# A convolution and attention hybrid on one core: the spectral mixer's lag blocks, regrouped by half of the tokens

## The reference, cut to what matters

```python
# phi: (tokens, 16 filters), causal convolution of u with each filter k
U_plus  = causal_conv(phi[:, k], u)                 # (b, t, k, d)
U_minus = sgn * causal_conv(phi[:, k], u * sgn)     # sgn = +1, -1, +1, ...
out  = einsum('btkd,k,kde->bte', U_plus,  sigma**0.25, M_phi_plus)
out += einsum('btkd,k,kde->bte', U_minus, sigma**0.25, M_phi_minus)
out += sum(shift(u, i) @ M_u[i] for i in range(3))
```

## Time and profile before

| | us |
|---|---|
| median of 3 runs | 216.42 (215.61 to 217.93) |
| profiled execution, device time | 216.58 |
| its span (first to last instruction) | 214.8 |
| PE / DVE / ACT / POOL busy | 186.6 / 154.1 / 97.3 / 39.2 |
| mean granted clock of TensorE over the span | 0.96 of full speed |

### The profile page before, as it was taken

One profiled execution on the slowest core, in us unless ns is written; L12 is line 12 of the kernel. 1 busy time (PEld: TensorE's weight loads), 2 busy tenths in 40 slices (PEclk: granted clock), 3 DMA queues, 4 the chain that ended last, 5 costly groups with the idle time before them and its releaser, 6 DMA issues.

```text
span 214.8 us, 6817 instructions
## 1 busy us (share of the span) xinstructions
PE 186.6 (87%) x2969; PEld 136.4 (64%) x2969; DVE 154.1 (72%) x347; ACT 97.3 (45%) x239; POOL 39.2 (18%) x57
## 2 busy tenths in 40 slices
PE   7999989899997989974898798598499969979994
PEld 2677668899997889721344684244147737735993
DVE  2789997958999999869777166595768749646101
ACT  3734997478888778511003350200868510035100
POOL 4970000012421440540100301133000000110000
PEclk9999999999999999999699999969955999999999
DMA  6830426345455510000143140001200190000000
GB/s 180 285 117 5 154 95 201 107 133 197 150 158 166 180 49 3 4 0 5 22 159 99 27 110 0 0 5 32 67 25 3 25 366 22 0 0 0 3 0 24
DMA packets 9042, 17.07 MB, mean 79 GB/s; under 512 B 2504, under 2 KB 3752, under 8 KB 8884
## 3 DMA queue, kind: packets, MB, share of 16 engines
q1 hardware_dynamic: 8868, 16.34, 24.1%
q10 hardware_dynamic: 144, 0.30, 0.4%
HBM read 16.20 MB, written 0.42 MB: 77 GB/s over the span
## 4 chain that ended last, share of the span: by engine, by line
PE 57%; DVE 26%; issue 6%; ACT 5%; POOL 2%; DMA 2%; POOLq 1%; DVEq 0%
PE ps L1540 55%; DVE onehot L1068 5%; POOL rstd L578 2%; DVE dots L1094 2%; DMA cst<-in_cst 2%; DVE arena L453 2%; DVE att L1118 1%; ACT arena L641 1%; DVE stu_fq L1443 1%; ACT onehot L837 1%; ACT table L641 1%; ACT arena L858 1%; DVE dots L1100 1%; DVE arena L1524 1%; DVE arena L1048 1%
## 5 line engine op out<-in xcount | busy, mean ns | idle before, releaser
L1540 PE MATMUL ps<-table,onehot 128*128 128x64 bf16 x1728 | 52.9, 194 | 5.0 <-issue 2.8
L1540 PEld LDWEIGHTS ps<-table,onehot 128*128 128x128 bf16 x1728 | 51.5, 98 | 6.5 <-issue 4.8
L1540 PE MATMUL ps<-spare 128*128 128x512 bf16 (+1 forms) x128 | 36.6, 419 | 8.1 <-DVE rexp L1359 2.3
L725 ACT ACTIVATE arena<-ps 128x512 f32<-128x512 f32 (+1 forms) x40 | 21.5, 553 | 14.2 <-PE ps L1540 13.9
L1540 PEld LDWEIGHTS ps<-spare 128*128 128x128 bf16 x128 | 12.4, 109 | 24.4 <-issue 6.8
L453 POOL TENSOR_TENSOR arena<-arena,w4p 128x288 f32<-128x288 f32 x21 | 16.2, 803 | 57.9 <-DVE arena L453 57.8
L1540 PE MATMUL ps<-arena 128*32 128x66 f32 (+4 forms) x388 | 25.2, 281 | 0.2 <-DVE arena L1320 0.2
L1540 PEld LDWEIGHTS ps<-arena 128*32 128x32 f32 (+2 forms) x388 | 22.2, 156 | 4.1 <-issue 1.4
L578 POOL TENSOR_TENSOR rstd<-var_eps,cst 128x4 f32<-128x4 f32 (+2 forms) x9 | 8.8, 982 | 82.7 <-DVE var_eps L937 56.1
L641 ACT ACTIVATE arena<-ps 128x512 f32<-128x512 f32 (+3 forms) x16 | 7.0, 469 | 26.1 <-PE ps L1540 20.3
L1068 DVE TENSOR_SCALAR onehot<-indexb,cst 128x2304 bf16<-128x2304 bf16 (+1 forms) x24 | 17.7, 771 | 0.0
(11 more groups left out here) (280 smaller groups left out, 305.0 us busy)
## 6 DMA issues: line engine op xcount, KB each, us to landing
indexb<-index_rows SPq DMA_DIRECT2D x20, 288.0 KB, 3.3
stu_fq<-index_rows SPq DMA_DIRECT2D x8, 288.0 KB, 3.4
arena<-in_toep SPq DMA_DIRECT2D x1, 2120.5 KB, 9.6
l<-in_l SPq DMA_DIRECT2D x1, 646.5 KB
stu_fq<-in_stu SPq DMA_DIRECT2D x1, 560.0 KB, 3.8
onehot<-in_l3w SPq DMA_DIRECT2D x1, 512.0 KB
table<-stu_mixed SPq DMA_DIRECT2D x4, 128.0 KB, 2.2
l<-in_l SPq DMA_DIRECT2D x1, 384.0 KB, 7.3
```

The lines of the kernel that those rows point to most:

```text
L725: nc.scalar.activation(gv[:, b % 2, :, at:at + count, :], ps[:, SB[n % len(SB)], 0:count * SLOT].rearrange("p (s a d) -> p a s d", s=count ...
L1540: return nc.tensor.matmul(out_ap, lhsT, rhs, start=start, stop=stop)
```

## The change

- **Values.** `projected` writes them in another arrangement: the partitions hold two groups of 8 filters (s = 0, 1) by 64 tokens, the columns the early and the late half of the tokens by 8 filters. Instead of 4 products (32 rows x 128 columns of weights, 512 moving columns) there are 16 (32 rows x 64 columns of weights, 256 moving columns): two halves by two groups by four images. The same values reach the same banks, and the copies keep their shapes.
- **Early tokens.** One 128x128 block now holds two filters' 64 early rows, so ODD, EVEN and BOTH each take 8 products where they took 16.
- **Late tokens.** They reach late results only, through a 64-column slice of the block (the lags of late to late are those of early to early). `add_late` issues two products of 128 rows x 64 columns: pair j to the partitions 64 to 127 of bank 4, pair j+1 to the partitions 0 to 63 of bank 1 (`LATE_BANK`). 4 such pairs each for ODD, EVEN and BOTH.
- **Joining.** ScalarE copies bank 1 (64 x 256) to SBUF (`late_rows`, a new last step of `a6`), and a product with a 64x64 identity adds it to the upper partitions of bank 4, between BOTH and the taps.
- **`toep`** is half as large and comes by three DMAs instead of one.

```diff
--- before.py
+++ after.py
@@ -210,9 +210,11 @@
         taps_v = arena[:, 2048:2048 + K2 * P]
         taps_q, taps_k = (arena[:, 2048 + at * P:2048 + (at + K2 - TAPS) * P] for at in (K2, 2 * K2 - TAPS))
         warm = sb("warm", [P, 1])
+        PAIRS, EARLY = NF // 2, P // 2
         fk, vcs = arena[:, 0:4096], arena[:, 4096:4096 + T * HG * 4 * HCOLS]
         v_sum, v_diff = arena[:, 0:NF * N], arena[:, NF * N:2 * NF * N]
-        ar_v, toep = arena[:, 8192:8192 + KU * N], arena[:, 8960:8960 + NF * LAGS + XT]
+        ar_v, toep = arena[:, 8192:8192 + KU * N], arena[:, 8960:8960 + PAIRS * LAGS + P]
+        late_rows = arena[0:EARLY, 11264:11264 + N]
         att_ch, y1, x2, ctx_n, qc, kc, vt, ln_ch, x4d, x5p = (
             arena[:, 12416 + i * N:12416 + (i + 1) * N] for i in range(10))
         vt1 = arena[:, 14976:14976 + T * (C + 1)].rearrange("p (n c) -> p n c", c=C + 1)
@@ -343,8 +345,8 @@
         PROJECTED = ("diff_even", "sum_even", "sum_odd", "diff_odd")
         v6 = Steps(sem("vector_stu"), "sum0 cen0 sq0 var0 eps0 sum1 cen1 ln0 sq1 var1 eps1 ln1 rows1 taps2 taps3 "
                    + " ".join(f"{n}{b}" for n in PROJECTED for b in (2, 3)) + " x6a x6")
-        a6 = Steps(sem("scalar_stu"), "x5p0 x5p1 rows0 taps0 taps1 " + " ".join(f"{n}{b}" for n in PROJECTED for b in (0, 1)))
-        t6 = Steps(sem("tensor_stu"), "parity0 parity1 turn0 turn1 taps " + " ".join(PROJECTED) + " out")
+        a6 = Steps(sem("scalar_stu"), "x5p0 x5p1 rows0 taps0 taps1 " + " ".join(f"{n}{b}" for n in PROJECTED for b in (0, 1)) + " late")
+        t6 = Steps(sem("tensor_stu"), "parity0 parity1 turn0 turn1 taps " + " ".join(PROJECTED) + " late out")
 
         block = ctx.enter_context(nc.Block())
 
@@ -559,7 +561,10 @@
                 sp.dma_start(heads_of[1][second, :], turn_d[0:NHEAD, N:N + DH]).then_inc(d_den, 16)
 
             sp.wait_ge(t5.sem, t5["kv3"])
-            sp.dma_start(toep, toep_d).then_inc(d_toep, 16)
+            for s in range(2):
+                sp.dma_start(toep[s * EARLY:(s + 1) * EARLY, 0:PAIRS * LAGS],
+                             toep_d[0:EARLY, s * PAIRS * LAGS:(s + 1) * PAIRS * LAGS]).then_inc(d_toep, 16)
+            sp.dma_start(toep[:, PAIRS * LAGS:], toep_d[:, NF * LAGS:NF * LAGS + P]).then_inc(d_toep, 16)
 
             sp.wait_ge(v6.sem, v6["x6"])
             sp.dma_start(out, x6t).then_inc(d_out, 16)
@@ -890,6 +895,8 @@
                 act.wait_ge(t6.sem, t6[name])
                 for b in (0, 1):
                     copy(by_parity_and_image(values)[:, r, b], ps[:, banks[b], :].rearrange("p (k e) -> p k e", k=NF), a6, f"{name}{b}")
+            act.wait_ge(t6.sem, t6["late"])
+            copy(late_rows, ps[0:EARLY, 1, 0:N], a6, "late")
 
 
         @block.vector
@@ -2030,8 +2037,13 @@
             def projected(name):
 
                 _, r, at, banks = PLACES[name]
-                for b, rows in IMAGES:
-                    ins = mm(ps[:, banks[b], :], tokens[rows, r, :], stu_w[rows, at:at + NF * D])
+                filters = PAIRS * D
+                for half in range(2):
+                    for s in range(2):
+                        for b, rows in IMAGES:
+                            ins = mm(ps[s * EARLY:(s + 1) * EARLY, banks[b], half * filters:(half + 1) * filters],
+                                     tokens[rows, r, half * EARLY:(half + 1) * EARLY],
+                                     stu_w[rows, at + s * filters:at + (s + 1) * filters])
                 ins.then_inc(t6.sem, t6.step(name))
 
             def taken(name):
@@ -2052,22 +2064,42 @@
                 return mm(ps[:, 4, to], lags, values, **{"start": False, "stop": False, **kw})
 
 
-            pe.wait_ge(d_toep, 16)
-            for k in range(NF):
-                at = k * LAGS
-                if k == NF // 2:
+            def add_late(pair, to, lag, values, at, **kw):
+
+                for j, rows, bank in ((pair, slice(EARLY, P), 4), (pair + 1, slice(0, EARLY), LATE_BANK)):
+                    first = j * LAGS + lag
+                    value = values[:, (PAIRS + j) * N + at.start:(PAIRS + j) * N + at.stop]
+                    ins = mm(ps[rows, bank, to], toep[:, first:first + EARLY], value,
+                             **({"start": False, "stop": False, **kw} if bank == LATE_BANK else {"start": False, "stop": False}))
+                return ins
+
+            LATE_BANK = 1
+            pe.wait_ge(d_toep, 48)
+            for j in range(PAIRS):
+                at = j * LAGS
+                if j == PAIRS // 2:
                     taken("sum_even")
                     pe.wait_ge(a6.sem, a6["sum_odd0"])
                     projected("diff_odd")
-                add(ODD, toep[:, at + P + 1:at + LAGS], v_diff[:, k * N:k * N + P], start=k == 0)
+                add(ODD, toep[:, at + P + 1:at + LAGS], v_diff[:, j * N:j * N + P], start=j == 0)
             taken("sum_odd")
+            for pair in range(0, PAIRS, 2):
+                add_late(pair, ODD, P + 1, v_diff, EVEN, start=pair == 0)
             taken("diff_odd")
-            for k in range(NF):
-                at = k * LAGS
-                add(EVEN, toep[:, at + P:at + LAGS - 1], v_diff[:, k * N + P:(k + 1) * N])
-                add(BOTH, toep[:, at:at + P], v_sum[:, k * N:(k + 1) * N])
-
-            at, taps = NF * LAGS, [ar_v[:, i * N:(i + 1) * N] for i in range(KU)]
+            for j in range(PAIRS):
+                at = j * LAGS
+                add(EVEN, toep[:, at + P:at + LAGS - 1], v_diff[:, j * N + P:(j + 1) * N])
+            for pair in range(0, PAIRS, 2):
+                add_late(pair, EVEN, P, v_diff, ODD)
+            for pair in range(0, PAIRS, 2):
+                ins = add_late(pair, BOTH, 0, v_sum, BOTH, stop=pair == PAIRS - 2)
+            ins.then_inc(t6.sem, t6.step("late"))
+            for j in range(PAIRS):
+                add(BOTH, toep[:, j * LAGS:j * LAGS + P], v_sum[:, j * N:(j + 1) * N])
+            pe.wait_ge(a6.sem, a6["late"])
+            mm(ps[EARLY:P, 4, BOTH], ident[0:EARLY, 0:EARLY], late_rows, start=False, stop=False)
+
+            at, taps = PAIRS * LAGS, [ar_v[:, i * N:(i + 1) * N] for i in range(KU)]
             shift = toep[:, at:at + P]
             add(BOTH, ident, taps[0])
             add(ODD, ident, taps[1][:, EVEN])
```

## The result

| | before | after |
|---|---|---|
| median, 20 runs each | 215.79 us (213.76 to 217.93) | 214.11 us (211.0 to 217.76) |
| ratio | | 0.9875, interval 0.9841 to 0.9909 |
| profiled execution, device time / span | 216.58 / 214.8 | 212.78 / 211.0 |
| PE / DVE / ACT busy | 186.6 / 154.1 / 97.3 | 179.3 / 154.0 / 97.4 |

The time lay inside my range (213.7 to 217.1). The ratio did not do what I held likeliest: I had put 0.60 on a change within 1%, and it came out at 1.25%, its interval just clear of the 0.991 that my 1.94 us make. The ratios of this document leave out runs over 1.5% above the fastest of the same kernel, which here kept 10 of the 20 new runs (mean 212.5 us) and, applied to the listed times, 15 of the 20 old ones (mean 215.4 us). The means over all 20 are 214.28 and 215.89 us, a difference of 1.61 us or 0.75%.

The account below looks back on a forecast made before the run. PE's stream was taken to bound the mixer to its end. The main sum's -2.07 us and +0.13 us ahead of it made -1.94 us: 214.6 us profiled, median 214.5 us, 8-in-10 range 213.7 to 217.1 us.

Parts of the forecast that it names:

- a change within 1%: Whole kernel: measured time neither faster nor slower than before by over 1% (2.16 us); chance 0.60.
- my 1.94 us: Whole kernel: net saving forecast, 2.07 us less in the main sum against 0.13 us more before ODD.
- main sum: Mixer, from the start of ODD to that of the taps: 15.43 us before, 13.36 us after, 2.07 us less.
- the taps' load: End of the main sum: the taps' first weight load, hidden before, now follows another layout and costs 0.11 us.
- Ahead of ODD: Mixer before ODD: changed layout after the taps, shorter load and eight tile starts, net +0.13 us.
- near 210.1: End of the mixer: time in us at which DVE's window product should stand in the changed kernel's timeline.
- pair slot of 128 columns: Late products: two 64-weight-column products side by side, taken at 0.111 us, possible 0.108 to 0.23 us; no trace row.
- a: PE stream: price of one slot of 128 moving columns, 0.111 us.
- 8a + 8b: Late EVEN and late BOTH: eight slots of 128 columns (0.111 us each) and eight of 256 (0.217 us each).
- 1.4 us more: Late groups: each of 24 steps exposes its 0.06 us weight load, giving 216.0 us; part of a smaller-gain rival, chance 0.13.
- an estimated 0.6 us: Each projection: 24 more passes at some 60 cycles each, giving 216.3 us; part of a smaller-gain rival, chance 0.13.
- The waits: Mixer: copies before `diff_odd` and EVEN stay covered, the former by some 0.2 us; bank 1's copy costs nothing; no wait added.

Follow-up runs that it names:

- held: Changed kernel with ten more products on the spare tile in linear attention, to keep TensorE busy; ratio to the kernel before 0.989 (0.984 to 0.994), mean 213.69 us.

## Why the prediction was right and wrong

**The main sum was right, term by term.** Forecast and start-to-start reading of the profile after, in us: ODD 1.09 and 1.09; `diff_odd` 1.06 and 1.06; ODD and late ODD 2.12 and 2.11; EVEN, late EVEN and late BOTH 4.74 and 4.73; BOTH 3.67 and 3.65; add-back 0.57 and 0.57; the taps' load 0.11 and 0.11 (206.50 to 208.20 is 1.70 us, 210.41 to 212.00 was 1.59). Together 13.36 and 13.32. Ahead of ODD the start moved by 0.13 and 4.37 - 4.19 = 0.18 us. Net 1.94 and 1.93, so to 0.01 us partly by luck: the two parts are off by 0.04 and 0.05 us and cancel. The window product came at 208.20 us and not near 210.1, because the mixer began 1.87 us earlier.

**The bounds.** The pair slot of 128 columns, for which the trace had no row, costs a, the value that I took. Late EVEN and late BOTH fit 8a + 8b with their loads hidden, and 32 passes went by in 1.05 us. The Trainium skill (TensorE: Matmul & The Clock Gate, the list on overlap ahead of "Measured speedup vs the span model") says that a weight load overlaps only products of another row group; the trace disagrees, since the late groups, which would then have taken 1.4 us more, came within 0.01 us of the sum without it. The Trainium skill (TensorEngine Tiling (Array Packing), "Instruction Overhead") gives each matmul some 60 cycles; read as a cost that adds up, that was an estimated 0.6 us for the 24 more passes of a projection, and `diff_odd` became 0.02 us shorter (1.08 to 1.06).

**The waits.** Neither `diff_odd` nor EVEN waited for a copy: the last VectorE copy ended at 196.90 us, EVEN's load began at 197.55. ScalarE's copies of `diff_odd` ended at 196.69. The copy of bank 1 took 0.38 us and ended at 202.78, and the product that needs it came at 205.93. The clock was 1.00 over the mixer:

```profile
188.90:208.20 19.30, 18.52 (x250) 14.03 (x250) 5.68 (x10) 5.16 (x11) 0.00 (x0) 1.00 0.01 2
```

The small loads took 0.55 to 0.59 us each to issue instead of 0.35, with nothing behind them.

**What failed is the step from the sum to the chances.** It held a change within 1% likeliest (0.60) on the ground that "one per cent is 2.16 us, about what a measurement can tell", with the runs' scatter taken from three runs. The measurement told a change from none well below that: 20 runs a side gave an interval of 0.34% to either side, about 0.7 us, and my own 1.94 us is well clear of it. On the other hand one set of runs does not fix a ratio to 0.1%: the same pair of kernels gave 0.9875, 0.994 and 0.993. My 0.9% stood a tenth of a per cent from the 1% line, so which side the measurement fell on was for the scatter to decide; that the time lay inside my range says nothing for the 0.60. The changed kernel's three sets of runs each spread with a standard deviation of 1.7 to 2.1 us, because the clock falls at different places in stages that the change doesn't touch. The trace of before had the reason in it: a mean granted clock of 0.96, with falls at three places, and I read that only for what it says about the mixer. The 0.8 us between the forecast and the recorded ratio (1.25% is 2.7 us) were not found in any mechanism: the mixer gives 1.93 us in all three profiles of the changed kernel, the means of the same first 40 runs 1.61 us, all runs together 1.6 (1.0 to 2.3), and two repetitions 0.6% and 0.7%. What makes the clock fall in one run and not in another stays open. That the runs give rather 0.3 us less than the mixer is inside their interval; a small effect outside the mixer, of either sign, is not excluded by them.

## What to carry to other kernels

Price a stream by starts of groups, with a slot for each count of moving columns and one sum for first load and change of layout; here that gave each group to 0.02 us. Halving the blocks pays only if the halves run side by side, and each change between layouts costs 0.14 to 0.20 us with its load, so gather the narrow products in one group. Before giving chances about one per cent, look at how often the clock falls in stages that the change leaves alone: three profiles of the changed kernel began the mixer at 188.54, 188.92 and 192.68 us.

## What the runs showed of the hardware

Eight float32 tiles of 32 rows by 64 columns stream at the pace of four tiles of 32 by 128 (32 passes of 256 columns in 1.05 us, 8 of 512 in 1.08), and 64-column products side by side in two banks lose nothing to each other (88 passes in 10.40 us, in one place 13.86). With two waits of TensorE filled by spare products the granted clock stayed at 1.00 over them and fell after the next gap: at 160 us in `held`, where it fell between 154 and 157 us in the profiles of the changed kernel and of the kernel before; mean clocks of whole runs rose from at most 0.976 to as much as 0.992.
